# Two 16-wide cross attentions: ones rows filled later, masks copied by two engines, key pieces sent one by one, a third value slot

## What is computed

```python
def _L3_xattn_ref(query_modal, key_value_modal, Wq, bq, Wk, bk, Wv, bv, Wo, bo):
    NUM_HEADS, HEAD_DIM = 16, 16
    q = _split_heads(query_modal @ Wq.T + bq)
    k = _split_heads(key_value_modal @ Wk.T + bk)
    v = _split_heads(key_value_modal @ Wv.T + bv)
    scores = jnp.einsum('bhnd,bhmd->bhnm', q, k) * HEAD_DIM ** (-0.5)
    attn = jax.nn.softmax(scores, axis=-1)
    x = jnp.einsum('bhnm,bhmd->bhnd', attn, v)
    return x.transpose(0, 2, 1, 3).reshape(query_modal.shape) @ Wo.T + bo

x = x + _L2_xattn_ref(_layernorm(x), ctx_1024, ctx_1024, ...)   # layer 2
x = x + _L3_xattn_ref(_layernorm(x), ctx_1024, ...)             # layer 3
```

## Time and profile before

| | us |
|---|---|
| median of 3 runs | 3737.07 |
| lowest and highest | 3736.17, 3737.77 |
| the profiled execution | 3736.93 |
| its span, from first to last instruction | 3735.1 |
| PE, DVE, ACT, POOL busy in it | 3387.2, 2206.9, 1508.6, 905.0 |
| granted PE clock, mean over the span | 0.962 of 2.4 GHz |

### The profile page before, as it was taken

One profiled execution on the slowest core, in us unless ns is written; L12 is line 12 of the kernel. 1 busy time (PEld: TensorE's weight loads), 2 busy tenths in 40 slices (PEclk: granted clock), 3 DMA queues, 4 the chain that ended last, 5 costly groups with the idle time before them and its releaser, 6 DMA issues. The chain is left out here.

```text
span 3735.1 us, 55585 instructions
## 1 busy us (share of the span) xinstructions
PE 3387.2 (91%) x22089; PEld 2086.9 (56%) x22108; DVE 2206.9 (59%) x3363; ACT 1508.6 (40%) x2233; POOL 905.0 (24%) x666
## 2 busy tenths in 40 slices
PE   8989998999999999999779898899988889997679
PEld 6855695655656556556535675344456544444245
DVE  4335314555554555555378515899763389985964
ACT  2335211433334333343356331467744147774321
POOL 1042001525335254263337212000030300000420
PEclk9999999999999999999989899899999989998889
DMA  5258462000000000000387445656201566640010
GB/s 189 101 199 268 170 248 79 7 6 4 6 1 28 36 4 10 4 4 1 47 310 249 147 161 150 149 117 129 51 26 36 177 162 125 128 82 22 0 48 34
DMA packets 228855, 346.83 MB, mean 93 GB/s; under 512 B 104176, under 2 KB 177584, under 8 KB 223984
## 3 DMA queue, kind: packets, MB, share of 16 engines
q1 hardware_dynamic: 228208, 342.16, 31.7%
q0 software_dynamic: 384, 1.05, 0.1%
HBM read 257.15 MB, written 86.02 MB: 92 GB/s over the span
## 5 line engine op out<-in xcount | busy, mean ns | idle before, releaser
L1412 POOL TENSOR_TENSOR L1x_acc<-L1x_acc,L1x_pr 128x512 f32<-128x512 f32 x256 | 418.0, 1633 | 135.7 <-ACT L1x_pr L1596 117.3
L1596 ACT ACTIVATE L1x_pr<-L1x_pss 128x1024 f32<-128x1024 f32 x272 | 278.4, 1024 | 288.2 <-PE L1x_pss L1506 280.5
L1642 DVE TENSOR_TENSOR L1x_acc<-L1x_acc,L1x_pr 128x512 f32<-128x512 f32 x256 | 255.5, 998 | 213.1 <-ACT L1x_pr L1596 209.3
L1228 DVE TENSOR_REDUCE L2x_pk<-L2x_psm 128x1 f32<-128x512 f32 x512 | 329.1, 686 | 36.9 <-PE L2x_psm L1060 30.9
L1228 DVE TENSOR_REDUCE L3x_pk<-L3x_psm 128x1 f32<-128x512 f32 x512 | 328.9, 686 | 33.1 <-PE L3x_psm L1060 26.7
L1620 DVE TENSOR_REDUCE L1x_pk<-L1x_psm 128x2 f32<-128x1024 f32 x144 | 168.0, 1167 | 212.3 <-PE L1x_psm L1444 212.3
L1205 ACT ACTIVATE L2x_pr<-L2x_pss 128x1024 f32<-128x1024 f32 x256 | 248.1, 1021 | 108.0 <-PE L2x_pss L1101 107.8
L1205 ACT ACTIVATE L3x_pr<-L3x_pss 128x1024 f32<-128x1024 f32 x256 | 248.1, 1021 | 104.4 <-PE L3x_pss L1101 104.2
L1506 PE MATMUL L1x_pss<-L1x_Q,L1x_K 64*128 64x256 f32 x2176 | 279.3, 376 | 0.0
L1465 PE MATMUL L1x_pss<-L1x_cT,L1x_w 128*128 128x512 f32 (+1 forms) x576 | 256.4, 584 | 1.9 <-DMA L1x_cT<-normed_context 1.9
L1470 PE MATMUL L1x_pss<-L1x_w,L1x_cT 128*128 128x256 f32 x1088 | 257.5, 387 | 0.0
(11 more groups left out here) (730 smaller groups left out, 6058.0 us busy)
## 6 DMA issues: line engine op xcount, KB each, us to landing
f0e_wt<-in_f_pieces SPq DMA_DIRECT2D x10, 3072.0 KB, 11.5
offset_rows<-s_rows SPq DMA_DIRECT2D x32, 768.0 KB, 5.9
L2x_KS<-L2x_key_parts SPq DMA_DIRECT2D x24, 1024.0 KB, 13.0
L3x_KS<-L3x_key_parts SPq DMA_DIRECT2D x24, 1024.0 KB, 13.0
s_add<-offset_rows SPq DMA_DIRECT2D x32, 512.0 KB, 7.4
n_cT<-in_ctxT SPq DMA_DIRECT2D x32, 512.0 KB, 4.6
f1e_wt<-in_f_pieces SPq DMA_DIRECT2D x8, 2048.0 KB, 12.5
L2x_key_parts<-n_kst SPq DMA_DIRECT2D x32, 384.0 KB, 2.8
```

The lines of the kernel that those rows point to most:

```text
L1228: nc.vector.reduce_max(pk[:, n % 2, h * QT + qt, j:j + 1], psm[:, x % 3, :], AX).then_inc(turn_read, 1)
L1412: i = nc.gpsimd.tensor_tensor(acc[:, n, 1, :, :], acc[:, n, 1, :, :], pr[:, A % RING, :, 1, :], ALU.add)
L1596: nc.scalar.activation(pr[:, A % RING, :, :, :].rearrange("p h e q -> p (h e q)"), pss[:, x:x + 2, :].rearrange("p h n -> p (h n)"), ACT.E ...
L1642: i = nc.vector.tensor_tensor(acc[:, n, 0, :, :], acc[:, n, 0, :, :], pr[:, A % RING, :, 0, :], ALU.add)
```

## The change

It has four parts, all in `narrow_attention`.

- POOL waits for `sel_in`, that is for DVE's cast of the pick table, before it fills the two rows of ones.
- The six mask copies behind the first two are shared: the three with an even number go to DVE (counted by `masked`), in its program ahead of all peaks, the three with an odd number stay on ACT (`masked_more`). PE's waits follow: picked(i) with i >= 4 waits for the copy of i - 2 on the engine that makes it; the first peaks of units 1 to 3, and the first value product, wait for both engines' copies.
- `stack` takes the pieces that it is to send. Piece 0, 1 and 2 of unit 0 are issued behind the stores of chunk 4, 5 and 6; before, all three ahead of the store of chunk 4. Units 1 to 7 keep all three together.
- `vst` has three slots, with a semaphore each. To make room, `rec` (reciprocals, used in the last unit) becomes a view of `pick_in`. The rows of semaphore numbers of a stage grow from 38 to 40.

```diff
-    CHUNK, CRING, SRING = 512, 4, 2
+    CHUNK, CRING, SRING = 512, 4, 3
-        rec = u.sb(pre + "_rec", [P, 2, S])
+        rec = pick_in[:, :, :].rearrange("p (n x) q -> p n (x q)", n=2)
-            def stack(n):
+            def stack(n, which=range(3)):
...
-                for x, parts in enumerate((of_half[:, 0:2], of_half[:, 0:2], of_half[:, 0:3:2])):
+                for x in which:
+                    parts = (of_half[:, 0:2], of_half[:, 0:2], of_half[:, 0:3:2])[x]
                     sp.dma_start(into[2 * hd * x:2 * hd * (x + 1)], parts).then_inc(ks_in[n % 2], 16)
...
             for j in range(NCH):
                 if j + CRING < NCH:
                     context(j + CRING)
-                if j == NCH - CRING:
-                    stack(0)
                 sp.wait_ge(v_ev, PER // 2 * (j + 1))
                 sp.dma_start(Vd[0][:, j * PER:(j + 1) * PER, :],
                              vst[:, j % SRING, :, :, :].rearrange("p t h e -> p t (h e)")).then_inc(v_outs[j % SRING], 16)
+                if NCH - CRING <= j < NCH - 1:
+                    stack(0, [j - NCH + CRING])
             for x in range(SRING):
-                sp.wait_ge(v_outs[x], 16 * NCH // SRING)
+                sp.wait_ge(v_outs[x], 16 * len(range(x, NCH, SRING)))
...
             pool.wait_ge(ones_in, 1)
+            pool.wait_ge(sel_in, 1)
             nc.gpsimd.memset(KS[ONE:ONE + 1, 0, :, :], 1.0).then_inc(ones_rows, 1)
...
                     elif n < NU:
-                        pe.wait_ge(masked_more, 2 * n)
+                        pe.wait_ge(masked, n + 2)
+                        pe.wait_ge(masked_more, n)
...
-                if i >= 4:
-                    pe.wait_ge(masked_more, i - 3)
+                if i >= 4 and i % 2:
+                    pe.wait_ge(masked_more, (i - 3) // 2)
+                elif i >= 4:
+                    pe.wait_ge(masked, i // 2 + 1)
...
-                    pe.wait_ge(masked_more, 2 * NU - 2)
+                    pe.wait_ge(masked, NU + 1)
+                    pe.wait_ge(masked_more, NU - 1)
...
-            for i in range(2, 2 * NU):
+            for i in range(3, 2 * NU, 2):
                 act.wait_ge(sel_mm, i + 1)
-                nc.scalar.copy(QM[:, i // 2, i % 2, :], pss[:, 2 + i % 2, :]).then_inc(masked_more, 1)
+                nc.scalar.copy(QM[:, i // 2, 1, :], pss[:, 3, :]).then_inc(masked_more, 1)
...
+            for i in range(2, 2 * NU, 2):
+                dve.wait_ge(sel_mm, i + 1)
+                nc.vector.tensor_copy(QM[:, i // 2, 0, :], pss[:, 2, :]).then_inc(masked, 1)
             read_peaks(0, 0, NP)
```

More of the change, by code:

```diff
@@ L31 @@
 NH = 16
-ROOM = 38
+ROOM = 40
 NUMBERS = {}
@@ L924, in narrow_attention @@
     names = ("w_here wv_here q_mm q_act part1 part2 sel_mm sel_in masked masked_more scratch_out qs_in kh_in0 kh_in1 ks_in0 ks_in1 v_in0 v_in1 cleared ones_rows ones_in "
-             "c_here0 c_here1 c_here2 c_here3 v_mm v_ev v_out0 v_out1 turn turn_read peak scored exps averaged o_copied chain").split()
+             "c_here0 c_here1 c_here2 c_here3 v_mm v_ev v_out0 v_out1 v_out2 turn turn_read peak scored exps averaged o_copied chain").split()
     with Tensors(nc) as u, stage(nc, *[pre + "_" + n for n in names]) as (block, *sems):
         (w_here, wv_here, q_mm, q_act, part1, part2, sel_mm, sel_in, masked, masked_more, scratch_out, qs_in, kh_in0, kh_in1, ks_in0, ks_in1, v_in0, v_in1, cleared,
-         ones_rows, ones_in, c_here0, c_here1, c_here2, c_here3, v_mm, v_ev, v_out0, v_out1, turn, turn_read, peak, scored, exps, averaged, o_copied, chain) = sems
-        kh_in, ks_in, v_in, c_here, v_outs = (kh_in0, kh_in1), (ks_in0, ks_in1), (v_in0, v_in1), (c_here0, c_here1, c_here2, c_here3), (v_out0, v_out1)
+         ones_rows, ones_in, c_here0, c_here1, c_here2, c_here3, v_mm, v_ev, v_out0, v_out1, v_out2, turn, turn_read, peak, scored, exps, averaged, o_copied, chain) = sems
+        kh_in, ks_in, v_in, c_here, v_outs = (kh_in0, kh_in1), (ks_in0, ks_in1), (v_in0, v_in1), (c_here0, c_here1, c_here2, c_here3), (v_out0, v_out1, v_out2)
         qscratch = nc.dram_tensor(pre + "_query_parts", (3, KC, P, T), BF16, kind="Internal").ap()
```

## The result

| | before | after |
|---|---|---|
| median (lowest to highest, 5 runs each, side by side) | 3737.07 (3733.31 to 3738.02) | 3716.18 (3710.0 to 3722.76) |
| ratio to before, 95% interval | | 0.9946 (0.9933 to 0.9959) |
| profiled execution | 3736.93 | 3710.0 |
| its span | 3735.1 | 3708.2 |

The gain is 20.9 us by the medians, and 15.3 to 25.0 by the interval; the forecast was 18.3, to 3718.8. The two profiled executions are 26.9 us apart, more than the medians: the one of the kernel after is the fastest of its five.

What follows compares the result with a forecast made beforehand. The prediction took VectorE as pacemaker of L2x and L3x, with idle time ahead of their units as the path. 9.34 + 8.98 - 0 = 18.3 us gave 3718.8 us, range 3714 to 3725.5.

Steps and rivals of the forecast that it cites:

- The bound: In L2x and L3x VectorE sets the pace; only its idle time ahead of the steady units is worth removing.
- Part 1: Stage front: ones rows filled behind the pick table's copy; picks up to 3.46 us earlier, worth 0.
- The cover: Stage front: first value product waits for the row selector's load, landing 2299.5, not for masks, done 2297.9.
- Part 2: Stage front: six mask copies shared by ScalarE and VectorE, done well before the selector lands; worth 0.
- Part 3: Value phase: three value slots remove the wait for chunk 4's store; 9.34 us in L2x, 8.98 in L3x.
- Part 4: End of value phase: single key pieces delay V, which still lands 0.9 us before the first average; charged 0.
- The clock: Behind the value phase PE's clock, 0.60, was left unchanged; lower end opened by 4 us for a possible saving.
- The V rival: Before the first averages V comes late, 6.6 us less gain: 3725.4; chance 0.13.
- the exchange of one stall for another: End of value phase: an equal wait, keys or V late by 9 us, replaces the stall: 3737; chance 0.08.
- the slower case: Key pieces behind stores cost 9.8 us each, V lands 4.7 us after the average's old start: 3746.5; chance 0.03.
- The paying front: First value product follows the masks, so 3.46 us more come in each stage: 3711.9; chance 0.06.

Runs made afterwards that it cites:

- front_only: Kernel before with only the ones rows filled behind the pick table's copy and the masks shared by two engines: 3737.07 us, 1.0001.
- pieces_only: Kernel before with only the three key pieces moved behind the stores of chunks 4, 5 and 6, still two value slots: 3715.46 us, 0.9943.
- slots_only: Kernel before with only a third value slot, the key pieces still together ahead of the store of chunk 4: 3720.46 us, 0.9948.
- the kernel with the early selector alone: Kernel after, with the loads of value bias and row selector issued right behind the value weights: 3705.8 us, 0.9921.

## Why the prediction was right

**The bound.** VectorE's idle time ahead of the units was the path: without the stall the first average came 9.8 us earlier in L2x and 7.9 in L3x. How much of it was there at the end of the stage differed, since the units changed too: 16.1 and 6.0 us in the kernel after, 14.2 and 7.5 with the slots only, 16.1 and 4.8 with the pieces only.

**Part 1, worth 0**, held. The copy cost 0.43 us (0.65 taken). The first picks came at 2283.64 against 2291.00, 7.4 us earlier, of which 3.9 is the stage's earlier start: 3.5, as forecast. The first value product stayed within 0.2 us of the selector's landing (2288.56 + 6.7 = 2295.3, against 2295.47), and front_only gave 1.0001. The cover was named rightly: take it away, and the front brings the first value product 4.7 us earlier without the stall, and shows in the time even with it (0.9979, against 0.9999 and 1.0001 for each edit alone).

**Part 2, worth 0**, held, and nothing could be told of it even uncovered.

**Part 3, 9.34 and 8.98 us.** Measured 9.3 and 8.6 in the value phases. What was wrong is to whom it was given. The prediction let the slots take the stall away and the pieces cost something; pieces_only brings all of it without a third slot, since store 4 ahead of the pieces lands 2.8 us after its issue and slot 0 is free in time. And slots_only shows that the third slot needs no earlier store, since the later wait holds up no work.

**Part 4, charged 0, slack 0.9 us.** The landings give rounds of 6.2 and 6.6 us against 6.65, V 0.73 us ahead of its reader, and a wait as soon as a piece was added. From the landing of store 5 (2335.1) to that of piece 1 (2340.1) it was 5.0 us, from store 6 (2342.6) to piece 2 (2346.7) 4.1, and V was in time. The prediction took from the Trainium skill (SBUF — State Buffer, Door 1: The DMA port swizzle) the 189 GB/s measured at 1 MiB, which makes a piece 5.5 us (an estimate). The same row of that table gives about 218 GB/s as the asymptote, free of a transfer's fixed time, which makes it 4.8 us (an estimate): the 4.8 at which the pieces landed in the full queue before agree with that.

**The clock.** The 4 us at the lower end were not needed: 0.3 us less from the maximum to the first average in L2x, 0.1 more in L3x.

**What was missed** is that the units change too, by PE's stands and the clock behind them: 4.7 us less in L2x's unit 1, 1.6 less in the rest of L2x's units, 1.9 more in L3x's. With 17.8 from the value phases and 0.1 lost in the fronts and behind the maximum, this gives the 22.1 that the profiled executions show in the two stages. The median gain of 20.9 lies between this and the forecast of 18.3. The term that was forecast is right in mechanism and in size; that the total came within 2.6 us of it is in part luck, since nothing in the sum stood for the units' 4.4.

The V rival (3725.4), the exchange of one stall for another (3737) and the slower case (3746.5) all needed a wait that the profile after doesn't have. The paying front (3711.9) needed a first value product 3.5 us earlier, and it came at the old place.

## What to carry to other kernels

Before widening a ring of buffers, look at what the release is queued behind: here sending the small store ahead of the bulk loads was enough, with the buffers there were. A change "worth nothing" under a cover can be worth something when the cover goes, so name the load that covers it, price the pair, and move that load next. And when a stall is gone, the next thing late stood here in the same timeline with its slack in tenths of a microsecond: work the chain of landings out, and send earlier what it ends with.

## What the runs showed of the hardware

- A cast of 128 x 512 from SBUF to SBUF took 9.46 us beside a fill of one partition on GpSimd, and 0.43 us without it, a factor of 22; mask copies out of PSUM beside the same kind of fill kept their 0.69 us. The trace agrees with the Trainium skill, SBUF — State Buffer, Who interferes with whom: VectorE and GpSimd share a port pair under an exclusive lock.
- A load of 64 KB took 6.7 us, behind other transfers, nearly as long as one of 1088 KB (7.4). Issued 10 us earlier (10.8 us into L2x instead of 21.3), it took 9.7 us, landed at 20.5 and was not waited for.
- A store of 544 KB landed 2.8 us after its issue ahead of the pieces, and 17.4 us after it behind three pieces of 1 MB.
- PE can stand 2.7 to 3.0 us for nothing that the profile shows, while large transfers run. Behind it the granted clock fell in some executions (to 0.50 to 0.68 over 5 us) and the unit of 64 peaks took 48.0 to 49.5 us; in others it stayed at 1.00, and the unit took 46.5 to 47.0; without the stand most units took 43.4 to 44.6. In L2x's unit 1 the stand came and went with edits elsewhere, and it is as large as many effects that one wants to measure.
- Useless matmuls kept the granted clock at 1.00 from 2340 to 2355 us, where it was 0.54 in the kernel with the early selector alone. That was worth 2.3 us a stage from the first scores to the first average.
